# Cross attention: two half-filled head groups put together by VectorE, and an output product over two groups in place of four

## The reference

```python
x = x + _L0_xattn_ref(_layernorm(x), ctx_512, ctx_512, Wq, bq, Wk, bk, Wv, bv, Wo, bo)

# _L0_xattn_ref, 16 heads of 16 features (the second one has no biases)
qh = (q @ Wq + bq).reshape(B, LQ, HEADS, D_K).transpose(0, 2, 1, 3)
kh = (k @ Wk + bk).reshape(B, LKV, HEADS, D_K).transpose(0, 2, 1, 3)
vh = (v @ Wv + bv).reshape(B, LKV, HEADS, D_K).transpose(0, 2, 1, 3)
scores = jnp.einsum('bhqd,bhkd->bhqk', qh, kh) * scale
attn = jax.nn.softmax(scores, axis=-1)
out = jnp.einsum('bhqk,bhkd->bhqd', attn, vh)
return out.transpose(0, 2, 1, 3).reshape(B, LQ, D_MODEL) @ Wo + bo
```

## Time and profile before

| | us |
|---|---|
| median of 3 runs | 3746.14 (3738.89 to 3748.32) |
| time of the profiled execution | 3732.94 |
| its span, first to last instruction | 3730.9 |
| PE busy | 3454.5 (93%) |
| PE weight loads busy | 2890.5 (77%) |
| DVE busy | 2511.4 (67%) |
| ACT busy | 2216.9 (59%) |
| POOL busy | 1473.9 (40%) |

### The profile page before, as it was taken

The page is one execution under the profiler, slowest core; times in us unless marked ns, Lnnn a source line. Parts: engine busy times, 40 slices in busy tenths (PEclk is TensorE's granted clock), DMA queues, the critical chain, the costliest instruction groups (busy, mean ns, idle before and its releaser), DMA issues. The chain is left out here.

```text
span 3730.9 us, 135338 instructions
## 1 busy us (share of the span) xinstructions
PE 3454.5 (93%) x58130; PEld 2890.5 (77%) x58131; DVE 2511.4 (67%) x4356; ACT 2216.9 (59%) x3479; POOL 1473.9 (40%) x1409
## 2 busy tenths in 40 slices
PE   9999999999794799989999999999879899999988
PEld 6888888888684566668888888887358788888967
DVE  5777777777544122168677777775689788888864
ACT  5666666666552122146666666666767877778632
POOL 4433333333033000055333333331068788888600
PEclk9999999999996899979999999999979999999989
DMA  2000100000007100111000001000011111111100
GB/s 82 30 30 30 39 30 30 30 30 21 11 1 280 37 30 31 55 53 51 30 30 30 30 30 39 30 21 28 4 37 46 40 42 42 43 42 43 35 25 22
DMA packets 60156, 148.22 MB, mean 40 GB/s; under 512 B 8210, under 2 KB 28466, under 8 KB 59218
## 3 DMA queue, kind: packets, MB, share of 16 engines
q1 hardware_dynamic: 56530, 131.57, 10.9%
q0 software_dynamic: 3072, 8.39, 0.7%
HBM read 123.15 MB, written 16.78 MB: 38 GB/s over the span
## 5 line engine op out<-in xcount | busy, mean ns | idle before, releaser
L799 ACT ACTIVATE x_probs<-x_score_ps 128x1024 f32<-128x1024 f32 (+1 forms) x896 | 814.9, 961 | 633.7 <-PE x_score_ps L625 626.0
L904 DVE TENSOR_REDUCE x_maxes<-x_misc_ps 128x1 f32<-128x512 f32 (+1 forms) x1792 | 1020.6, 626 | 29.7 <-PE x_misc_ps L543 25.2
L2448 POOL TENSOR_TENSOR b_drive<-b_b_all,b_dtx 128x1024 f32<-128x1024 f32 x256 | 602.7, 2369 | 307.5 <-DVE b_dtx L2542 176.3
L836 POOL CAST x_kT_hi<-x_kT 128x512 fp32r<-128x512 f32 (+1 forms) x448 | 254.3, 568 | 1154.4 <-ACT x_kT L702 1060.7
L2505 DVE TENSOR_TENSOR_SCAN b_state<-b_decay_ps,b_drive 128x512 f32<-128x512 f32 x512 | 602.9, 1214 | 45.7 <-issue 19.9
L619 PE MATMUL x_score_ps<-x_qz,x_kT 32*128 32x128 f32 x13312 | 589.8, 277 | 1.3 <-issue 0.9
L619 PEld LDWEIGHTS x_score_ps<-x_qz,x_kT 32*128 32x128 f32 x13312 | 500.2, 182 | 4.2 <-issue 1.8
L590 PE MATMUL x_misc_ps<-x_probs,x_v 128*32 128x64 f32 x26624 | 464.7, 221 | 0.0
L590 PEld LDWEIGHTS x_misc_ps<-x_probs,x_v 128*32 128x32 f32 x26624 | 392.4, 110 | 77.8 <-issue 38.5
L2279 PE MATMUL b_acc_ps<-ident,b_read 128*128 128x128 f32 x3072 | 417.2, 282 | 16.9 <-DVE b_xc L2528 16.9
L543 PE MATMUL x_misc_ps<-x_kT_hi,x_qz_hi 32*128 32x512 f32 (+1 forms) x2048 | 425.2, 404 | 5.6 <-DVE x_u L949 2.2
(11 more groups left out here) (316 smaller groups left out, 5903.3 us busy)
## 6 DMA issues: line engine op xcount, KB each, us to landing
x_raw<-in_ctxT SPq DMA_DIRECT2D x64, 800.5 KB, 4.5
b_b_all<-b_b_rows SPq DMA_DIRECT2D x128, 256.0 KB, 3.3
m_w<-in_m_w SPq DMA_DIRECT2D x16, 704.0 KB, 20.2
m_w<-in_m_w SPq DMA_DIRECT2D x8, 768.0 KB, 21.5
m_slot_rows<-m_zero SPq DMA_DIRECT2D x1, 4992.0 KB, 17.6
m_block_rows<-m_slot_rows SPq DMA_DIRECT2D x39, 128.0 KB, 2.0
m_slot_out<-m_out SPq DMA_DIRECT2D x39, 128.0 KB, 1.7
x<-in_x SPq DMA_DIRECT2D x4, 512.0 KB, 6.6
```

The costliest lines, as they stand in the source:

```text
L799: nc.scalar.activation(probs[rows, s % 2, js, 0:n], score_ps[rows, js, 0:n], ACT.Exp).then_inc(exp_done, 1)
L904: nc.vector.tensor_reduce(maxes[:, c:c + m, j, k0 // NB], bank(op)[:, 0:m * even].rearrange("p (c k) -> p c k", c=m)[:, :, 0:kn], AX.X, AL ...
L2448: nc.gpsimd.tensor_tensor(drive[:, h % 3, :, :], b_all[:, k % 2:k % 2 + 1, :].broadcast_to([P, 2, NB]), dtx[:, half * 2:half * 2 + 2, :], ...
```

## The change

- `v_sb` has four slots of 16 columns for each pair of heads: values of the even head, ones, ones, values of the odd head. An even head's weights are slots 0 and 1 as before, an odd head's are slots 2 and 3: its ones stand in front. Matmuls in `weigh` are as many and as large. ACT writes the values with an access pattern of one more dimension; POOL sets the ones in runs of 32 columns.
- `spread_sums` becomes `part_sums`, at the same place. It swaps the two halves of each 32 partitions of `u_sb` (one shuffle of the same size), and puts together, with the two columns of `mask` (1 and 0 for the two halves), the values of the even head and of the odd head into `weighed` (128 x 2 groups x 64), and likewise the sums into `sums`. That is two tensor_scalar and two scalar_tensor_tensor of 128 x 128 elements each.
- There is one reciprocal of 128 x 128, at g = 2, in place of two; `divide` is 128 x 128 in place of 128 x 256 and stands at g = 3 in place of g = 4.
- `wo` and `bv` are no longer padded: `project_out` and `bias_row` have two matmuls in place of four, and the DMA of `wo` is 256 KB in place of 512 KB.
- Three more semaphores.

```diff
-        wo_sb = sb(f"{tag}_wo", [P, GROUPS, D])
-        bv_sb = sb(f"{tag}_bv", [P, GROUPS])
+        wo_sb = sb(f"{tag}_wo", [P, KD, D])
+        bv_sb = sb(f"{tag}_bv", [P, KD])
...
-        v_sb = sb(f"{tag}_v", [P, NG, 2, H, 2 * DH])
+        v_sb = sb(f"{tag}_v", [P, NG, 2, H // 2, 4, DH])
...
             def project_out(op):
                 dst = open_bank(op)
                 pe.wait_ge(w_in, 16 * NW)
                 pe.wait_ge(o_done, 2 * op[1] + 2)
-                for r in range(GROUPS):
+                for r in range(KD):
                     ins = nc.tensor.matmul(dst[:, 0:D], oT[:, r, :, :].rearrange("p b q -> p (b q)"), wo_sb[:, r, :],
-                                           start=r == 0, stop=r == GROUPS - 1)
+                                           start=r == 0, stop=r == KD - 1)
...
-                                v_sb[0:keys(i), g, h, 8 * c + 2 * j + half, :], probs[0:keys(i), s % 2, j, at:at + LQ],
+                                v_sb[0:keys(i), g, h, 4 * c + j, 2 * half:2 * half + 2, :].rearrange("p s d -> p (s d)"), probs[0:keys(i), s % 2, j, at:at + LQ],
...
-                    v_sb[rows, g, 0:n, :, 0:DH].rearrange("p a h d -> p (a h) d"),
-                    bank(op)[rows, 0:n * D].rearrange("p (a d) -> p a d", d=DH), ACT.Copy).then_inc(act_free, 1)
+                    v_sb[rows, g, 0:n, :, 0:4:3, :].rearrange("p a h s d -> p (a h) s d"),
+                    bank(op)[rows, 0:n * D].rearrange("p (a s d) -> p a s d", s=2, d=DH), ACT.Copy).then_inc(act_free, 1)
...
-            def spread_sums(b):
+            def part_sums(b):
 
                 read_out(dve, ("P", b * NG + NG - 1))
-                nc.vector.stream_shuffle(sums[:, :], u_sb[:, b % 2, :, :].rearrange("p r q -> p (r q)"),
-                                         [DH] * (P // QUADS)).then_inc(sums_done, 1)
...
+                nc.vector.stream_shuffle(swapped[:, :, :].rearrange("p r q -> p (r q)"),
+                                         u_sb[:, b % 2, :, :].rearrange("p r q -> p (r q)"),
+                                         [(n + DH) % (2 * DH) for n in range(P // QUADS)]).then_inc(swap_done, 1)
+                nc.vector.tensor_scalar(upper[:, 0, :, :], odd, mask[:, 1:2], None, ALU.mult).then_inc(upper_done, 1)
+                dve.wait_ge(swap_done, b + 1)
+                nc.vector.tensor_scalar(upper[:, 1, :, :], odd_swapped, mask[:, 1:2], None, ALU.mult).then_inc(upper_done, 1)
+                dve.wait_ge(upper_done, 2 * b + 1)
+                nc.vector.scalar_tensor_tensor(weighed[:, :, :], even, mask[:, 0:1], upper[:, 0, :, :], ALU.mult, ALU.add
+                                               ).then_inc(weighed_done, 1)
+                dve.wait_ge(upper_done, 2 * b + 2)
+                nc.vector.scalar_tensor_tensor(sums[:, :, :], even_swapped, mask[:, 0:1], upper[:, 1, :, :], ALU.mult, ALU.add
+                                               ).then_inc(sums_done, 1)
 
-            def invert(b, half):
+            def invert(b):
                 dve.wait_ge(sums_done, b + 1)
...
-                nc.vector.reciprocal(recip[:, of], sums[:, of]).then_inc(recip_done, 1)
+                nc.vector.reciprocal(recip[:, :, :], sums[:, :, :]).then_inc(recip_done, 1)
...
-                if g in (2, 3) and u > 0:
-                    invert(u - 1, g - 2)
-                if g == 4 and u > 0:
+                if g == 2 and u > 0:
+                    invert(u - 1)
+                if g == 3 and u > 0:
                     divide(u - 1)
```

More of the change, by code:

```diff
@@ L417, in cross_attention @@
         u_sb = sb(f"{tag}_u", [P, 2, GROUPS, LQ])
-        oT = sb(f"{tag}_oT", [P, GROUPS, 2, LQ])
-        sums = sb(f"{tag}_sums", [P, GROUPS * LQ])
-        recip = sb(f"{tag}_recip", [P, GROUPS * LQ])
+        oT = sb(f"{tag}_oT", [P, KD, 2, LQ])
+        swapped = sb(f"{tag}_swapped", [P, GROUPS, LQ])
+        upper = sb(f"{tag}_upper", [P, 2, KD, LQ])
+        weighed = sb(f"{tag}_weighed", [P, KD, LQ])
+        sums = sb(f"{tag}_sums", [P, KD, LQ])
+        recip = sb(f"{tag}_recip", [P, KD, LQ])
         bias = sb(f"{tag}_bias", [P, D])
@@ L436, in cross_attention @@
         exp_done = sem(f"{tag}_exp_done")
+        swap_done = sem(f"{tag}_swap_done")
+        upper_done = sem(f"{tag}_upper_done")
+        weighed_done = sem(f"{tag}_weighed_done")
         sums_done = sem(f"{tag}_sums_done")
@@ L865, in _ @@
             split_weights(pool, 1)
-            nc.gpsimd.memset(v_sb[:, :, :, :, DH:], 1.0).then_inc(filled, 1)
+            nc.gpsimd.memset(v_sb[:, :, :, :, 1:3, :], 1.0).then_inc(filled, 1)
             for n in range(AHEAD, NG):
@@ L914, in keep_shift, with halves @@
                 nc.vector.tensor_copy(shift[:, b % 2, :], bank(op)[:, 0:2 * P]).then_inc(dve_free, 1)
-            def spread_sums(b):
+            def halves(ap):
+                ap = ap.rearrange("p (c s) q -> p c s q", s=2)
+                return ap[:, :, 0, :], ap[:, :, 1, :]
+            def part_sums(b):
                 read_out(dve, ("P", b * NG + NG - 1))
-                nc.vector.stream_shuffle(sums[:, :], u_sb[:, b % 2, :, :].rearrange("p r q -> p (r q)"),
-                                         [DH] * (P // QUADS)).then_inc(sums_done, 1)
@@ L922, in _ @@
-            HALF = GROUPS * LQ // 2
-            def invert(b, half):
+                if b == 0:
+                    dve.wait_ge(q_in, 48)
+                even, odd = halves(u_sb[:, b % 2, :, :])
+                even_swapped, odd_swapped = halves(swapped[:, :, :])
+                nc.vector.stream_shuffle(swapped[:, :, :].rearrange("p r q -> p (r q)"),
+                                         u_sb[:, b % 2, :, :].rearrange("p r q -> p (r q)"),
+                                         [(n + DH) % (2 * DH) for n in range(P // QUADS)]).then_inc(swap_done, 1)
@@ L925, in invert @@
+                dve.wait_ge(upper_done, 2 * b + 2)
+                nc.vector.scalar_tensor_tensor(sums[:, :, :], even_swapped, mask[:, 0:1], upper[:, 1, :, :], ALU.mult, ALU.add
+                                               ).then_inc(sums_done, 1)
+            def invert(b):
                 dve.wait_ge(sums_done, b + 1)
-                of = slice(half * HALF, (half + 1) * HALF)
-                nc.vector.reciprocal(recip[:, of], sums[:, of]).then_inc(recip_done, 1)
+                nc.vector.reciprocal(recip[:, :, :], sums[:, :, :]).then_inc(recip_done, 1)
@@ L929, in divide @@
             def divide(b):
-                dve.wait_ge(recip_done, 2 * b + 2)
-                nc.vector.tensor_tensor(oT[:, :, b % 2, :], u_sb[:, b % 2, :, :],
-                                        recip[:, :].rearrange("p (r q) -> p r q", q=LQ), ALU.mult).then_inc(o_done, 1)
+                dve.wait_ge(weighed_done, b + 1)
+                dve.wait_ge(recip_done, b + 1)
+                nc.vector.tensor_tensor(oT[:, :, b % 2, :], weighed[:, :, :], recip[:, :, :], ALU.mult).then_inc(o_done, 1)
@@ L1037, in _ @@
                 if g == 1 and u > 0:
-                    spread_sums(u - 1)
+                    part_sums(u - 1)
             gather(("P", STEPS - 1))
-            spread_sums(B - 1)
-            for half in range(2):
-                invert(B - 1, half)
+            part_sums(B - 1)
+            invert(B - 1)
             divide(B - 1)
@@ L2848, in xattn @@
     def xattn(n, wq, wk, wv, wo, bq, bv):
-        def padded(v):
-            v = v.reshape(2, 4, 2, DH, -1).transpose(1, 3, 0, 2, 4).reshape(4, DH, 4, -1)
-            return np.concatenate([v, np.zeros_like(v)], axis=1).reshape(P, 4, -1)
         arr[f"x{n}_wq"] = wq.reshape(KD, P, D).transpose(1, 0, 2)
@@ L2855, in xattn @@
         arr[f"x{n}_wv"] = wv
-        arr[f"x{n}_wo"] = padded(wo)
-        arr[f"x{n}_bv"] = padded(bv if bv is not None else np.zeros(D, f)).reshape(P, 4)
+        arr[f"x{n}_wo"] = wo.reshape(KD, P, D).transpose(1, 0, 2)
+        arr[f"x{n}_bv"] = (bv if bv is not None else np.zeros(D, f)).reshape(KD, P).T
         arr[f"x{n}_bq"] = (bq if bq is not None else np.zeros(D, f)).reshape(KD, P).T
```

## The result

| | before | changed | ratio of changed to before, 95% interval |
|---|---|---|---|
| first comparison, median us | 3744.61 | 3769.66 | 1.0068 (1.0051 to 1.0086) |
| second comparison, on another occasion | 3737.40 | 3765.46 | 1.0075 (1.0060 to 1.0090) |
| profiled execution of the first | 3732.94 | 3767.17 | |

The change costs 25 to 28 us. Forecast were +18.7 us and 3764.8 us. The profiled execution of before was the fastest that was seen of it in the first comparison, so the distance of the two profiled executions (34 us) says too much.

What follows compares the result with a forecast made beforehand. PE was taken to bound the kernel: 31.7 us saved on PE against 50.4 us of K's delay gave +18.7 us, 3764.8 us on the median of 3746.14. The range of 8 in 10 was 3734 to 3795 us.

Steps and rivals of the forecast that it cites:

- PE bounds; a wait in its stream is lost time: Both attention loops: PE busy 855.5 of 860 and 922.6 of 930 us, so instructions removed gain time and waits lose it.
- VectorE has no slack at g = 2, and K is where it shows: At g = 2 K's weight load follows the first maximum by some 0.05 us, so added VectorE work delays K.
- Once per batch, 60 times, nothing taken back: 30 batches in each attention pay K's delay of 0.84 us once: 60 x 0.84 = 50.4 us.
- rival 1: At g = 1 PE takes back up to 0.49 us of the delay per batch: -10.7 us, 3735 us; chance 0.15.
- rival 2: At g = 2 VectorE's delay never reaches PE, leaving only the gain: -31.7 us, 3714 us; chance 0.10.
- The four operations at 0.21 us each, 0.84 us: Two tensor_scalar and two scalar_tensor_tensor behind the shuffle, before g = 2's first maximum, priced unchained; 0.84 us in all.
- Rival 3: POOL's product holds the first new operation behind the shuffle, 0.23 us on top: +32.5 us, 3779 us; chance 0.08.
- Rival 4: Each new operation behind the shuffle waits for the one before, 1.32 us: +47.5 us, 3794 us; chance 0.05.
- Rival 5: The clock falls in the new 0.84 us gap, costing tens of us or more; chance 0.02.
- W: 0.91 us each: Output product on PE, four of eight records removed: 0.91 us for each of 30 W inside the loops, 27.3 us.
- The chain of VectorE ahead of the last W, counted as nothing: At each attention's end, one reciprocal and part of the division saved offset four new operations within 0.3 us.

Runs made afterwards that it cites:

- e3: Kernel before with output product and bias row cut to their first two of four groups, VectorE's work unchanged; 3722.40 us beside 3749.42, ratio 0.9932.
- e4: Kernel before with two more scalar_tensor_tensor of 128 x 128, results unread, behind the shuffle; 3775.91 us beside 3749.42, ratio 1.0074.
- e2: Kernel before with its shuffle moved ahead of the gather at g = 1; 3751.63 us beside 3749.42, ratio 1.0006.
- e5: Changed kernel with GpSimd's product for the next batch's queries moved from g = 1 to g = 3; 3759.83 us, ratio 1.0063 to before.
- e8: Kernel before with two more scalar_tensor_tensor ahead of the gather at g = 1, shuffle left behind it; 3736.44 us beside 3737.40, ratio 0.9995.
- e1: Changed kernel with part_sums moved ahead of the gather of P at g = 1; 3714.64 us beside 3749.42, ratio 0.9906 to before.
- e7: The changed kernel run again, unaltered, as anchor; 3765.46 us beside 3737.40 for the kernel before, ratio 1.0075.

## Why the prediction was right, and where its sizes were off

- *PE bounds; a wait in its stream is lost time.* Right. e3 shows what is taken from PE as gain (25.5 us), e4 what is put in as loss (28 us).
- *VectorE has no slack at g = 2, and K is where it shows.* Right. K went from 1.56 to 2.56 us behind M, and e2 shows that nothing was to be had below 1.56.
- *Once per batch, 60 times, nothing taken back.* Right. The idle time ahead of K is 55.8 us in all, and rival 1 (return at g = 1) and rival 2 (VectorE's delay never reaches PE) fall with e4. The 0.49 us by which K was late at g = 1 came from one batch; over all batches K stands there 1.83 us behind M on the mean, some 0.26 later than elsewhere, and 1.82 in the changed kernel. Of the 0.98 us some 0.01 is given back there.
- *The four operations at 0.21 us each, 0.84 us.* Too small: it was 1.00 us in the batch shown, and more in two batches near the start of the first attention, where POOL's second operation lies there too. A tensor_scalar that nothing holds leads by 0.19 to 0.20 us, close to the price. The two scalar_tensor_tensor lead by 0.26 (301.30, 301.56, 301.83), not 0.21. I had priced them by the one row whose duration was like its neighbours' (0.29); here they took 0.34. And the first tensor_scalar lost 0.08 us to POOL. K was 0.98 us later on the mean, which makes 59 us for the 50.4 of the sum.
- *Rival 3 (POOL in the way)* came true beside the forecast, and smaller: 0.08 us in place of 0.23. The prediction let it pass because the first two operations have one tensor input each; e5 shows that it was just such an operation that was held. The operation ends 0.08 us after POOL's and not a whole 0.28 us after it, so most of its own time overlaps the wait, and it loses little. The rule of the Trainium skill that the prediction named ("SBUF — State Buffer", rule on the shared port pair) names tensor_scalar among the operations that can take the shared pair. By that rule the trace agrees that a tensor_scalar can be held, and the prediction read it too narrowly; for the price, the 0.08 us lost is less than a full block from POOL's end on would cost. The other rule of the Trainium skill ("VectorE: DVE Perf Modes", tier table), of twice the rate for tensor_scalar, is not decided: 0.19 us from start to start is less than the 0.21 of a tensor_tensor, though not by the 0.07 that was worked out from it.
- *Rival 4 (each waits for the one before, 0.33)* did not come: the steps were 0.20 and 0.26.
- *Rival 5 (the clock falls in the gap)* did not come: it stands at 1.00 in both windows.
- *W: 0.91 us each.* It was 0.87, as four records take 0.95 and not half of 1.82. The bias row gave 0.86 for 0.91 (47.21 to 48.17 in the changed kernel). The last W gave 1.87 and 1.44, 3.3 for 3.5.
- *The chain of VectorE ahead of the last W, counted as nothing.* Right: PE idles 3.38 us for it, as against 3.36.

With the sizes measured: 30 x 0.87 + 0.86 + 3.3 = 30.3 us gained, 60 x 0.98 = 59 us lost, +29 us. The two comparisons have +25 and +28, with intervals from 19 to 34. The forecast of +18.7 us was too low by 6 to 9 us, nearly all of it the price of the four operations. That the second comparison's 3765.46 us lies within 1 us of the forecast's 3764.8 is luck: the kernel before took 3737.40 us there, 8.7 less than the 3746.14 on which the forecast was built.

## What to carry to other kernels

An engine that is busy to 73% can still have no slack at one place: before giving it work, look in the timeline how long the bounding engine's start lies behind its release at that very place, and whether it starts later there than in steps where this release does not bind. Here the distance was 0.05 us and the start no later than elsewhere (1.56 us). Moving the release forward brought nothing (e2), work added ahead of it was paid nearly in full (e4), and the same work 2.3 us earlier, ahead of an operation that waits anyway, was free (e8). A change that saves on the bounding engine and adds on another should be written with the added work in the other's idle time: the two lines of e1 turned 25 to 28 us of loss into 32 to 35 us of gain.

## What was not expected of the hardware

- A scalar_tensor_tensor of 128 x 128 with a column as factor takes 0.34 to 0.35 us and leads the next operation by 0.26, in a stream where tensor_scalar of the same shape takes 0.28 and leads by 0.19 to 0.20. The one that stood elsewhere in the trace took 0.29.
- A VectorE tensor_scalar from SBUF to SBUF, with one tensor input, is held by a GpSimd product of two SBUF tensors. It ended 0.08 us behind it, at 0.36 us and in two early batches 0.77 us of duration, and took 0.28 with the product moved away. In e7, where the product ended 0.16 us or less behind its start, it kept its 0.27 us.
